# A two-layer cross-attention transformer on one core: maximum units beside the first scores of short steps, a layer's weight split spread over four passes, and bulk loads issued first

## What is computed

```python
h1 = _ln(x, n1_g, n1_b)
x = _attn(h1, h1, q1, k1, v1, o1_w, o1_b, heads) + x          # heads = 20, 16 columns each
h2 = _ln(x, n2_g, n2_b)
x = _attn(h2, context, q2, k2, v2, o2_w, o2_b, heads) + x
h3 = _ln(x, n3_g, n3_b)
proj = h3 @ ff_w1 + ff_b1
a, g = jnp.split(proj, 2, axis=-1)                            # 1280 columns each
ff = a * jax.nn.gelu(g, approximate=False) @ ff_w2 + ff_b2
return ff + x
```

## Time and profile before

| | us |
|---|---|
| median of 3 runs | 3419.41 |
| lowest, highest | 3409.3, 3423.13 |
| the profiled execution | 3420.76 |
| its span on the core | 3418.9 |

### The profile page before, as it was taken

The page is one execution under the profiler, slowest core; times in us unless marked ns, Lnnn a source line. Parts: engine busy times, 40 slices in busy tenths (PEclk is TensorE's granted clock), DMA queues, the critical chain, the costliest instruction groups (busy, mean ns, idle before and its releaser), DMA issues.

```text
span 3418.9 us, 43794 instructions
## 1 busy us (share of the span) xinstructions
PE 3089.5 (90%) x16000; PEld 1395.8 (41%) x16000; DVE 2057.7 (60%) x2732; ACT 1903.0 (56%) x3646; POOL 730.7 (21%) x972
## 2 busy tenths in 40 slices
PE   4887888989999999998999999999999998998998
PEld 1332333334344433544345343453434543453445
DVE  5555556766656666655665666566765676566521
ACT  1553556656664566555664556645666466645631
POOL 3332121312302132022320333112230014002000
PEclk8997989999999999999999999999999999999999
DMA  6443334432433334334343444333244214322212
GB/s 160 136 121 102 90 84 125 136 103 56 135 97 85 108 93 133 99 106 129 95 126 85 124 118 120 105 97 113 61 130 109 69 41 134 94 51 49 69 41 77
DMA packets 208597, 342.27 MB, mean 100 GB/s; under 512 B 25464, under 2 KB 107776, under 8 KB 207104
## 3 DMA queue, kind: packets, MB, share of 16 engines
q1 hardware_dynamic: 203264, 338.09, 35.7%
q0 software_dynamic: 5120, 1.39, 0.3%
HBM read 202.29 MB, written 114.75 MB: 93 GB/s over the span
## 4 chain that ended last, share of the span: by engine, by line
PE 65%; DVE 10%; DMA 10%; ACT 6%; POOL 4%; issue 3%; SPq 2%; DVEq 0%; ACTq 0%; POOLq 0%
PE pr L1278 14%; PE po L1295 13%; DVE mx L1086 7%; PE pd L1262 7%; PE pf L1145 5%; PE pf L1198 5%; PE pf L1211 5%; PE pf L1168 4%; ACT ET L995 3%; DMA QS<-MT 3%; PE pf L1186 3%; PE pf L1177 2%; DMA raw<-ff_w_dram 2%; DMA scr_k<-HS 2%; DMA WS<-parts 2%
## 5 line engine op out<-in xcount | busy, mean ns | idle before, releaser
L995 ACT ACTIVATE ET<-pr 128x512 f32<-128x512 f32 (+1 forms) x2720 | 1478.6, 597 | 1262.2 <-PE pr L1278 1244.7
L1086 DVE TENSOR_REDUCE mx<-pd 128x2 f32<-128x800 f32 (+2 forms) x1600 | 1607.8, 1031 | 935.8 <-PE pd L1262 931.6
L1278 PE MATMUL pr<-QS,KS 64*128 64x512 f32 (+1 forms) x2720 | 862.3, 505 | 154.6 <-ACT ET L995 85.9
L1262 PE MATMUL pd<-KS,QS 64*128 64x400 f32 (+2 forms) x3200 | 684.2, 379 | 86.1 <-DVE mx L1086 67.6
L1295 PE MATMUL po<-ET,V 128*32 128x512 f32 (+2 forms) x5440 | 751.9, 626 | 0.5 <-ACT OU L1001 0.5
L1278 PEld LDWEIGHTS pr<-QS,KS 64*128 64x128 f32 (+1 forms) x2720 | 332.1, 185 | 1028.7 <-ACT ET L995 714.0
L1262 PEld LDWEIGHTS pd<-KS,QS 64*128 64x128 f32 x3200 | 375.6, 193 | 158.7 <-DVE mx L1086 117.3
L871 POOL TENSOR_TENSOR HS<-uT,HS 128x512 fp32r<-128x512 f32 (+4 forms) x168 | 190.3, 1133 | 605.0 <-ACT uT L959 604.8
L888 POOL DMA_DIRECT2D QS<-MT x160 | 94.2, 590 | 904.6 <-DVE MT L1110 902.6
L1198 PE MATMUL pf<-HS,WS 128*128 128x512 f32 x665 | 191.5, 418 | 11.3 <-issue 8.0
L1295 PEld LDWEIGHTS po<-ET,V 128*32 128x32 f32 (+2 forms) x5440 | 107.2, 108 | 215.5 <-issue 198.6
(11 more groups left out here) (81 smaller groups left out, 2054.0 us busy)
## 6 DMA issues: line engine op xcount, KB each, us to landing
WS<-parts SPq DMA_DIRECT2D x160, 320.0 KB, 3.0
QS<-scr_q SPq DMA_DIRECT2D x80, 512.0 KB, 5.6
scr_k<-HS SPq DMA_DIRECT2D x144, 200.0 KB
scr_q<-HS SPq DMA_DIRECT2D x96, 256.0 KB
KS<-scr_k SPq DMA_DIRECT2D x80, 300.8 KB, 5.2
KS<-scr_k SPq DMA_DIRECT2D x80, 300.0 KB, 6.1
KS<-scr_k SPq DMA_DIRECT2D x80, 192.0 KB, 4.7
scr_k<-HS SPq DMA_DIRECT2D x48, 256.0 KB
```

The costliest lines, as they stand in the source:

```text
L995: activation(ET[0:q.rows[k], s % 2, 2 * pair + e, :], pr[e][0:q.rows[k], :], ACT.Exp).then_inc(score_free, 1)
L1086: v.reduce_max(mx[q.kind][:, t, 2 * p:2 * p + 2, c], pd[no % 2][:, :, 0:cols], AX_X).then_inc(unit_free, 1)
L1262: ins = mm(pd[no % 2][:, e, 0:cols], queries[:, t * P:(t + 1) * P], keys, start=True, stop=True)
L1278: mm(pr[e][0:m, :], keys, queries, start=True, stop=True).then_inc(score_ready, 1)
```

## The change

Four edits.

1. **Bulk loads first.** SP issues them right behind the first scratch zeroing, ahead of the first stores and stagings.
2. **The split of layer 1** goes to passes 1 to 4, in parts of 6, 5, 5 and 5 places (`W_PARTS`), between the first twelve fills of each pass. It was 11 and 10 places in passes 3 and 4.
3. **Two v2a fills** stand ahead of t3, not one.
4. **The units' planner.** `all_first` tells whether a step has a short fill or none in beat 1 and none in beat 3. Such a step's units all go to beat 0 and none to beat 2. `LAST_UNIT_AHEAD` is 9.5, and a group's last unit must come six beats before its first step, or eight beats after its first unit became possible.

```diff
+W_PARTS = [(0, 6), (6, 11), (11, 16), (16, 2 * FM + 1)]
...
-        if c in (B - 1, B):
-
-            half = places("w", 1, 0, FM + 1) if c == B - 1 else places("w", 1, FM + 1)
+        if 0 < c <= len(W_PARTS):
+
             easy = 3 * TT
-            seq = mixed(seq[:easy], half) + seq[easy:]
+            seq = mixed(seq[:easy], places("w", 1, *W_PARTS[c - 1])) + seq[easy:]
         behind = places("v2a", c + 1)
         if c:
             first, rest = gate(c - 1, 4)
-            seq += behind[:1] + places("t3", c - 1) + places("g", c - 1) + [first] + rest
-            behind = behind[1:]
+            seq += behind[:2] + places("t3", c - 1) + places("g", c - 1) + [first] + rest
+            behind = behind[2:]
...
-LAST_UNIT_AHEAD, PUT_BEHIND, MOST_UNITS = 7.0, 0.5, 2
+LAST_UNIT_AHEAD, PUT_BEHIND, MOST_UNITS = 9.5, 0.5, 2
+
+BEATS_AHEAD, LEAST_BEATS = 6, 8
+
+
+SHORT_FILL = 0.9
+
+
+def all_first(step):
+    first, second = (sum(FILL_LENGTH.get(p[0], 0.0) for p in PLACES.get(4 * step + r, [])) for r in (1, 3))
+    return first < SHORT_FILL and not second
+
+
+def unit_places(beat):
+
+    if all_first(beat // 4):
+        return 2 if beat % 4 == 0 else 0
+    return 1 if beat % 2 == 0 else 0
...
+    if not unit_places(_b):
+        continue
     _now = AT[_b]
+    _next = AT[min(_b + 2 * unit_places(_b), BEATS - 1)]
...
+        if units_now(_n, _now):
+            _first_beat.setdefault(_n, _b)
+        if _n not in _first_beat:
+            continue
         _sum += units_now(_n, _now)
         _rate = max(_rate, _sum / max(UNITS_TO[_n] - _now, 0.5))
-        _need = max(_need, -(-_sum // max((4 * GROUPS[_n].step0 - 1 - _b) // 2, 1)))
-    _credit = min(max(_credit + _rate * (_now - _before), _need), max(_need, MOST_UNITS))
-    _before = _now
+        _last = max(4 * GROUPS[_n].step0 - BEATS_AHEAD, min(_first_beat[_n] + LEAST_BEATS, 4 * GROUPS[_n].step0))
+        _count = sum(unit_places(b) for b in range(_b, max(_last, _b + 2)))
+        _need = max(_need, -(-_sum * unit_places(_b) // _count))
+    _credit = min(max(_credit + _rate * (_next - _now), _need), max(_need, MOST_UNITS))
...
             set_scratch("q1", 0)
+            load_context(0)
+            load_x(1)
+            for which, what, l in LOAD_BEHIND[None]:
+                if which not in ("a", "b"):
+                    load_weights(which, what, l)
+            set_scratch("q1", 1)
+            for b in range(2, B):
+                load_x(b)
+            set_scratch("q2", 0)
+            set_scratch("q2", 1)
```

More of the change, by code:

```diff
@@ L400 @@
 _left = {q.n: len(q.units) for q in GROUPS[1:]}
-_credit, _before = 0.0, 0.0
+_credit, _first_beat = 0.0, {}
 for _b in range(0, BEATS, 2):
+    if not unit_places(_b):
+        continue
     _now = AT[_b]
+    _next = AT[min(_b + 2 * unit_places(_b), BEATS - 1)]
     _rate, _need, _sum = 0.0, 0, 0
     for _n in sorted(n for n in _left if _left[n]):
+        if units_now(_n, _now):
+            _first_beat.setdefault(_n, _b)
+        if _n not in _first_beat:
+            continue
         _sum += units_now(_n, _now)
         _rate = max(_rate, _sum / max(UNITS_TO[_n] - _now, 0.5))
-        _need = max(_need, -(-_sum // max((4 * GROUPS[_n].step0 - 1 - _b) // 2, 1)))
-    _credit = min(max(_credit + _rate * (_now - _before), _need), max(_need, MOST_UNITS))
-    _before = _now
+        _last = max(4 * GROUPS[_n].step0 - BEATS_AHEAD, min(_first_beat[_n] + LEAST_BEATS, 4 * GROUPS[_n].step0))
+        _count = sum(unit_places(b) for b in range(_b, max(_last, _b + 2)))
+        _need = max(_need, -(-_sum * unit_places(_b) // _count))
+    _credit = min(max(_credit + _rate * (_next - _now), _need), max(_need, MOST_UNITS))
     while _credit >= 1.0:
@@ L810, in _ @@
                     stage_group(q, part)
-                if beat == FIRST_BEAT:
-                    load_context(0)
-                    load_x(1)
-                    for which, what, l in LOAD_BEHIND[None]:
-                        if which not in ("a", "b"):
-                            load_weights(which, what, l)
-                    set_scratch("q1", 1)
-                    for b in range(2, B):
-                        load_x(b)
-                    set_scratch("q2", 0)
-                    set_scratch("q2", 1)
                 if ended(beat, MOVE, MOVE_ALONE):
```

## The result

| | before | after |
|---|---|---|
| median, us | 3420.89 | 3404.36 |
| lowest, highest | 3409.3, 3434.78 | 3390.45, 3412.28 |
| runs | 8 | 8 |
| the profiled execution | 3420.76 | 3404.07 |

The ratio is 0.9949, with a 95% interval of 0.9926 to 0.9971. That is 17 us gained (10 to 25), where 81 were forecast, and outside the range of 3295 to 3385.

A forecast was written before the change was run, and what follows sets the result against it. TensorE was taken to bound the kernel (65% of the chain), ScalarE and VectorE where they make it wait. Terms 6 + 32 + 9 + 17 + 20 + 19 = 103 gained, 22 lost: -81, so 3340 us; range 3295 to 3385.

The forecast's parts named there:

- Bulk loads: Start: bulk issued early lets the first group's put land in 1.9 us, not 7.6; 6 us gained, ends 0 and 8.
- Rival E: Start: the put passes the bulk, its slowness had another reason, so the start gains 0; 3346 us, chance 0.1.
- Earlier last units: Group starts: ten waits for maxima shrink, 32 us gained (18 to 41), plus 9 from fewer low-clock steps (0 to 12).
- The t3 place: t3 steps: one more v2a step covers ScalarE's 3.56 us wait for k2 stores; 17 us gained, ends 0 and 19.
- The split: Layer 1's split: places spread out, ScalarE no longer waits for raw weights; 20 us gained, ends 8 and 27.
- Short steps: Short attention steps: 109 go from units (1,1) to (2,0), saving 0.17 us each; 19 us gained, ends 5 and 22.
- Three units in one beat: First scores: a third unit waits for the first's reduction; +11 in short steps, sum +22 with long ones, ends 0 and 45.
- Rival B: Group starts and t3: the next wait takes the gains, half of 32 + 9 + 17 stays; 3369 us, chance 0.2.
- Rival A: Attention steps: two or more units in a row make TensorE wait for VectorE; slower, +55, 3476 us, chance 0.04.

The follow-up runs named there:

- u_early: Kernel before with the new planner's early ends only, no step treated as short: 3445.37 us, ratio 1.0065 to the kernel before.
- three_cap: Changed kernel with a short step's third unit moved to its second scores and bulk loads where they stood before: 3365.02 us, ratio 0.9839 to the kernel before.
- three_cap_late: three_cap with groups ended as late as before (7.0 us ahead, no beats ahead): 3384.11 us, ratio 0.9882 to the kernel before.
- p_v2a: Kernel before with only the second v2a fill ahead of t3: 3407.79 us, ratio 0.9957 to the kernel before.
- p_split: Kernel before with only the spread of layer 1's split: 3389.52 us, ratio 0.9908 to the kernel before.
- u_first: Kernel before with only short steps' units put at the first scores, groups ended as late as before: 3433.89 us, ratio 1.0033 to the kernel before.
- u_cap: Kernel before with the planner's whole change, but a short step's third unit at its second scores: 3408.81 us, ratio 0.9950 to the kernel before.
- p_units: Kernel before with only the units' planner changed: 3442.76 us, ratio 1.0056 to the kernel before.

## Where the prediction was right and wrong

- **Bulk loads** (6 gained, "I cost it at nothing"): wrong step. The landing was right: 1.9 us at a quiet queue. The forecast counted SP's issues, which do end before the first stores, at 30 us, but not their transfers: the DMA engines were full or nearly so until 40 us (shares 1.04, 0.92 and 1.00 in the three windows from 10 us on). The stores' issue went from 2.08 to 10.03 us, and the keys came 12 us late. Alone it is +2 (-3 to +7).
- **Rival E**, that the put passes the bulk, is not borne out: put and bulk apart, it landed in 1.9 us, not 7.6. The rule of the Trainium skill that gave it ("DMA: Bandwidth & Descriptors", "Queues, rings and completion order") does not by itself say that a small transfer is quick in full engines, and here it was not.
- **Earlier last units** (32 and 9 of clock): right on the waits named, 68.0 to 21.6 us. Wrong in taking them as gained. I asked what the later chain would be late for at the same group, and never which transfer the wait had covered. This is the step that failed most. At the seven starts of the table 32.6 us went and 26.1 came back at the next first unit, and u_early, early ends alone, is +22, and not -41. In good company (three_cap against three_cap_late) early ends gave some 15, little over the noise.
- **The t3 place** (17): p_v2a gave 15. The size is right, the make-up is not. t3 gave 15 (from 17.10, 16.50 and 16.10 to 11.6 each in the changed kernel), the t1 waits took back some 16 to 20, and unit waits elsewhere gave the rest. What the moved v2a fill had covered at its old place was not looked up.
- **The split** (20, ends 8 and 27): p_split gave 31 (23 to 40), over the end of the range by its median. The term was also summed wrongly: it took the 61.70 us of the earlier trace rows for eleven steps of pass 4, where ten took that and eleven took 64.95. Redone, 14.3 + 16.8 - 7.3 gives 24 and not 20. Against this the split of p_split has 19 of waits and casts and 10 of clock, for which the sum had no term here. So the mechanism was right, and that 19 meets 20 is in part luck.
- **Short steps** (0.17 us each, 19): the 3.15 us is exact. The tables have 113 such steps from step 40 on and not 109, which changes nothing. But with late ends it was worth nothing (u_first, +11), since the groups' chains don't shrink with the steps and 20 steps had a third unit.
- **Three units in one beat** (11 of 22): the mechanism was right, the size a third of what it is. It is 36 us for 46 units (u_cap), 34 in full company. Without a fill the step was as forecast, 3.51 us; with a short fill it was 4.29 to 4.64, not 4.05. The third unit was put at 0.7 us beside a short fill and took 1.0 to 1.1. And I credited 6 us for steps that had (2,2) before. Against (2,1), which is what the third unit could have had, my own lengths would have made 46 x 0.52 = 24.
- **Rival B**, the gain taken by the next wait, has the mechanism: it named the put and t3 as the places, though, and its 3369 was still 35 us too good. Rival A had the reason of the third units but put it on the (2,0) steps, which lose nothing.

The 64 us between forecast (-81) and measurement (-17), by the parts alone: bulk loads +8, t3 +2, split -11, planner +57 (from -38 to +19), and +8 that the parts lose together. Of the planner's 57, 36 - 11 = 25 are the third units, by u_cap. The other 32 are near the 36 us by which the idle time before first units rose in p_units (18.3 to 53.9). That these are one and the same is a sum that fits, and not a measurement.

## What to carry to other kernels

Before a wait is taken away, list what runs under it: the next transfer in line may be landing there, and then the wait only moves to its user. Units of work with two buffers went two in a row for nothing here. A third cost about the 1.0 us of a reduction where a short fill stood behind it, and 0.1 where none did. Change the planner's rule and the spots that it crowds together, and measure each part alone: here two parts of four carried the gain, and one cap on the third unit turned 17 us into 51. And before a run is said to rule out a queue, see in its trace that the issue has really moved.

## What the runs showed of the hardware that I had not expected

Issuing is not free of what is in flight: three stores that SP issued within 2.08 us took it 10.03 when the DMA engines were full (share 1.00 from 30 to 40 us). That lateness reaches TensorE when a staging stands behind the stores. And runs of one kernel differed by up to 31 us, mostly with the mean granted clock (0.951 to 0.960). In p_split 10 of 29 us came by the clock in the split above, so a change that removes waits may gain twice: the wait, and the slow steps behind it.
